# Attention in cycles of three score tiles, with the tiles for the maxima in a ring of four single PSUM banks

## The reference, cut to what matters

```python
B, T, C = x.shape                       # 4, 1024, 256
h = (x - mu) * rsqrt(var + 1e-05) * ln_gamma + ln_beta
qkv = (h @ w_qkv + b_qkv).reshape(B, T, 3, 16, 16)      # 16 heads of 16
scores = einsum('bhqd,bhkd->bhqk', q, k) / sqrt(16)
attn = softmax(scores, axis=-1)
out = einsum('bhqk,bhkd->bhqd', attn, v)
out = out @ w_out + b_out
return residual + out
```

## Time and profile before

| what | us |
|---|---|
| median of three runs | 1146.5 |
| the profiled execution | 1145.95 |
| its span, first to last instruction | 1143.9 |
| TensorE busy (1: busy time) | 1065.6 (93%) |
| VectorE busy | 999.5 (87%) |
| ScalarE busy | 808.9 (71%) |
| first tile for the maxima to last copy of `ps_o` | 104.4 to 785.6 |

### The profile page before, as it was taken

The page is one execution under the profiler, slowest core; times in us unless marked ns, Lnnn a source line. Parts: engine busy times, 40 slices in busy tenths (PEclk is TensorE's granted clock), DMA queues, the critical chain, the costliest instruction groups (busy, mean ns, idle before and its releaser), DMA issues.

```text
span 1143.9 us, 22167 instructions
## 1 busy us (share of the span) xinstructions
PE 1065.6 (93%) x8566; PEld 584.0 (51%) x8566; DVE 999.5 (87%) x1475; ACT 808.9 (71%) x1654; POOL 244.6 (21%) x345
## 2 busy tenths in 40 slices
PE   5997899999999999999999999997899998999995
PEld 4885333333333333333333333334667765888884
DVE  6786999999999999999999999943499998579887
ACT  4462388888888888888888888874567686343443
POOL 6421600000000000000000000102254333565643
PEclk9898699999999999999999999998999998899998
DMA  7595404413432440442243140212134325634321
GB/s 272 153 313 202 57 13 76 67 29 59 68 48 41 76 64 17 74 68 40 48 68 60 36 76 12 92 56 59 41 111 144 110 86 164 195 87 135 103 75 55
DMA packets 87332, 101.55 MB, mean 89 GB/s; under 512 B 21884, under 2 KB 57212, under 8 KB 87228
## 3 DMA queue, kind: packets, MB, share of 16 engines
q1 hardware_dynamic: 86396, 98.56, 36.2%
q10 hardware_dynamic: 832, 1.58, 0.4%
HBM read 55.09 MB, written 43.88 MB: 87 GB/s over the span
## 4 chain that ended last, share of the span: by engine, by line
PE 70%; DVE 14%; issue 3%; POOL 2%; ACT 1%; DMA 1%; SPq 0%; DVEq 0%; PEldq 0%; POOLq 0%; ACTq 0%
PE ps_o L785 25%; PE ps_s L773 19%; PE ps_m L762 10%; DVE maxes L705 3%; PE p_a L1330 3%; PE p_p L1756 2%; DVE p_q_c L1254 1%; DVE p_kv_c L1254 1%; PE p_a L1733 1%; DVE ln_stats L69 1%; PE p_t L1336 1%; DVE p_hid L81 1%; DVE zT_lo L2019 1%; PE p_p L1402 1%; DMA inverse<-inverse_sums 1%
## 5 line engine op out<-in xcount | busy, mean ns | idle before, releaser
L679 ACT ACTIVATE prob<-ps_s 128x512 f32<-128x512 f32 x1024 | 556.1, 597 | 117.8 <-PE ps_s L773 101.0
L705 DVE TENSOR_REDUCE maxes<-ps_m 128x2 f32<-128x1024 f32 x512 | 605.4, 1217 | 16.0 <-PE ps_m L762 12.7
L785 PE MATMUL ps_o<-prob,v_ones 128*32 128x256 f32 x4096 | 327.3, 391 | 7.6 <-issue 7.2
L773 PE MATMUL ps_s<-q_stack,k_stack 64*128 64x512 f32 x1024 | 260.6, 499 | 0.0
L762 PE MATMUL ps_m<-k_stack,q_stack 62*128 62x512 f32 x1024 | 218.9, 420 | 12.7 <-DVE maxes L705 9.0
L773 PEld LDWEIGHTS ps_s<-q_stack,k_stack 64*128 64x128 f32 x1024 | 98.8, 184 | 210.8 <-ACT prob L679 187.9
L785 PEld LDWEIGHTS ps_o<-prob,v_ones 128*32 128x32 f32 x4096 | 81.6, 108 | 191.5 <-issue 102.8
L638 POOL COPY v_ones<-v_all 128x512 f32<-128x512 f32 x16 | 9.9, 616 | 511.2 <-PE ps_o L785 511.2
L762 PEld LDWEIGHTS ps_m<-k_stack,q_stack 62*128 62x128 f32 x1024 | 100.8, 191 | 30.2 <-DVE maxes L705 23.1
L405 ACT ACTIVATE p_parts<-ps_qk,cols 128x512 fp32r<-128x512 f32 x32 | 22.0, 688 | 38.2 <-PE ps_qk L450 33.3
L1402 PE MATMUL p_p<-p_hT,w_p 128*128 128x512 f32 x96 | 42.7, 594 | 2.6 <-ACT p_hT L1167 2.6
(11 more groups left out here) (301 smaller groups left out, 1538.3 us busy)
## 6 DMA issues: line engine op xcount, KB each, us to landing
qk_parts<-p_parts SPq DMA_DIRECT2D x32, 512.0 KB, 7.2
q_stack<-qk_parts SPq DMA_DIRECT2D x96, 128.0 KB, 4.7
k_stack<-qk_parts SPq DMA_DIRECT2D x96, 128.0 KB, 7.7
oT<-o_sb SPq DMA_DIRECT2D x32, 256.0 KB, 4.2
x_all<-in_x_dram SPq DMA_DIRECT2D x8, 512.0 KB, 10.0
heads<-oT SPq DMA_DIRECT2D x16, 256.0 KB
inverse<-inverse_sums SPq DMA_DIRECT2D x16, 256.0 KB
out_dram<-x_all SPq DMA_DIRECT2D x7, 512.0 KB, 3.5
```

The costliest lines, as they stand in the source:

```text
L679: act.activation(prob[at % P_RING][:, h], ps_s[:, (GH * at + h) % S_RING], ACT.Exp, scale=HD ** -0.5).then_inc(exp_done, 1)
L705: dve.tensor_reduce(maxes[:, i // 2, i % 2], ps_m[:, i % M_PAIRS], AX.X, ALU.max).then_inc(m_taken, 1)
L773: pe.matmul(ps_s[:, (GH * (UNITS * slot + KT * qc + kt) + h) % S_RING], r32(k_st[slot][rows, pair, kt * P:(kt + 1) * P]), r32(q_st[slot][r ...
L785: ins = pe.matmul(ps_o[32 * h:32 * h + 32, queries], v_st[slot][:, kt, h], prob[(UNITS * slot + KT * qc + kt) % P_RING][:, h, queries], st ...
```

## The change

The work of attention is put into another order, and the two kinds of tiles are handled in other units.

- A cycle of TensorE now has three score tiles, three tiles for the maxima and three quarters of a block of products (`weigh` over 384 queries, or split over two blocks as 128 + 256 or 256 + 128), in the order s s m m s m, products. A half has ten such cycles and one of two tiles (`CYCLES` is 11, `tiles_of`). Products are those of two cycles earlier.
- `ps_m` is a ring of four single banks; TensorE waits for each tile, and VectorE reduces one bank (128 x 512 elements) with one instruction, 974 times; only in front of the loop, for 50 tiles, does it still take pairs (25 times). `maxima_through` turns a tile's number into the count of reductions.
- The rows of the array of the two kinds are swapped for the tiles for the maxima (`BASES[1 - i % 2]`), and `place_max` follows that.
- The chain of four small instructions of VectorE becomes: two maxima into `maxm` and `top`, a subtraction, a transpose. The signs change (the stack of keys gets -1 where it had 1). They are put behind the first, second and third reduction of the next half but one instead of following each other, and `maxes` has two buffers.
- The reciprocals, `take_o` (now after six exponentials of a half, before after four) and the steps of `begin_mixing` (now one in each cycle) take places in the new order.

```diff
-M_PAIRS = 2
-M_MMS = GH * (CHUNK // P) * (T // CHUNK)
-AHEAD = M_MMS // 2
+M_BANKS = 4
+TILES = GH * KT
+HALVES = NG * T // CHUNK
+CYCLES = TILES // 3 + 1
+LEAD = TILES + 18
+FIRST_PAIRS = LEAD // 2
+ALL_TILES = TILES * HALVES
+ALL_MAXIMA = FIRST_PAIRS + ALL_TILES - LEAD
+LAST_HALF = (ALL_TILES - LEAD) // TILES
+LAST_CYCLES = (ALL_TILES - LEAD) % TILES // 3 + 1
+
+def tiles_of(j):
+    return 3 if j < CYCLES - 1 else 2
+
+def maxima_through(tile):
+    return tile // 2 + 1 if tile < LEAD else FIRST_PAIRS + tile - LEAD + 1
...
+                        if half and GH * kt + h == 5:
+                            take_o(*divmod(half - 1, QC))
...
+            def take_max(tile, count):
+                half, i = divmod(tile, TILES)
+                bank = tile % M_BANKS
+                dve.wait_ge(m_ready, tile + count)
+                dve.tensor_reduce(maxes[half % 2][:, i:i + count], ps_m[:, bank:bank + count], AX.X, ALU.max).then_inc(m_taken, 1)
...
+            def whole_maxima(half):
+                dve.wait_ge(m_taken, maxima_through(TILES * half + TILES - 1))
+                for dst in (maxm[:], r32(top[:, 0])):
+                    dve.tensor_tensor(dst.rearrange("p (hp odd t) -> p hp t odd", hp=HP, odd=2), by_head(half)[:, :, :, 0], by_head(half)[:, :, :, 1],
+                                      ALU.max).then_inc(own, 1)
+
+            def low_parts(half):
+                dve.wait_ge(own, 3 * half + 2)
+                dve.tensor_tensor(top[:, 1], maxm[:], top[:, 0], ALU.subtract).then_inc(own, 1)
+
+            def turn_maxima(half):
+                g, qc = divmod(half, QC)
+                dve.wait_ge(own, 3 * half + 3)
                 dve.wait_ge(m_in[qc], 32 * g)
+                dve.transpose(topT[qc][:], top[:].rearrange("p a b -> p (a b)")).then_inc(m_turned, 1)
...
+            for half in range(HALVES):
+                for j in range(CYCLES):
+                    for tile in range(TILES * half + LEAD + 3 * j, TILES * half + LEAD + 3 * j + tiles_of(j)):
+                        if tile < ALL_TILES:
+                            take_max(tile, 1)
+                        if half + 1 < HALVES:
+                            past = tile - TILES * (half + 2)
+                            if past == 0:
+                                whole_maxima(half + 1)
+                            if past == 1:
+                                low_parts(half + 1)
+                            if past == 2:
+                                turn_maxima(half + 1)
+                    if half in (HALVES - 5, HALVES - 4) and j % 3 == 0:
+                        invert(4 * (half - (HALVES - 5)) + j // 3)
...
+            def fill_max(tile):
+                if tile >= M_BANKS:
+                    pe.wait_ge(m_taken, maxima_through(tile - M_BANKS))
+                score_for_max(tile, tile % M_BANKS).then_inc(m_ready, 1)
...
+            def weigh(half, first, count):
+                g = half // QC
+                while count:
+                    kt, at = divmod(first, GH)
+                    to = min(GH, at + count)
+                    n, queries = KT * half + kt, slice(at * P, to * P)
+                    if at == 0:
+                        pe.wait_ge(exp_done, GH * n + GH + S_RING)
+                        if kt == 0:
+                            pe.wait_ge(o_taken, half)
+                            pe.wait_ge(v_set, g + 1)
+                    for h in range(GH):
+                        ins = pe.matmul(ps_o[32 * h:32 * h + 32, queries], v_st[g % SLOTS][:, kt, h], prob[n % P_RING][:, h, queries],
+                                        start=kt == 0 and at == 0, stop=kt == KT - 1 and to == GH)
+                    if to == GH:
+                        ins.then_inc(pv_done, 1)
+                    first, count = first + to - at, count - (to - at)
...
+                for j in range(CYCLES):
+                    tile = TILES * half + LEAD + 3 * j
+                    score(half, 3 * j)
+                    score(half, 3 * j + 1)
+                    if tile + 1 < ALL_TILES:
+                        fill_max(tile)
+                        fill_max(tile + 1)
+                    if tiles_of(j) == 3:
+                        score(half, 3 * j + 2)
+                        if qc == 0 and tile + 2 == TILES * (half + 2) and tile + 2 < ALL_TILES:
                             pe.wait_ge(stack_in[nxt], STACK_LOADS * ((g + 1 - nxt) // 3 + 1))
+                        if tile + 2 < ALL_TILES:
+                            fill_max(tile + 2)
+                    slot = CYCLES * (half - LAST_HALF) + j - LAST_CYCLES
+                    if slot >= 0:
+                        begin_mixing(slot)
+                    weigh_cycle(half, j - 2)
```

More of the change, by code:

```diff
@@ L669, in take_o @@
                 act.activation(o_sb[qc][:], ps_o[:], ACT.Copy).then_inc(o_taken, 1)
[L671 to L689, removed]
+            for half in range(HALVES):
+                for kt in range(KT):
+                    n = KT * half + kt
+                    act.wait_ge(pv_done, n)
+                    for h in range(GH):
+                        act.wait_ge(s_ready, GH * n + h + 1)
+                        act.activation(prob[n % P_RING][:, h], ps_s[:, (GH * n + h) % S_RING],
+                                       ACT.Exp, scale=HD ** -0.5).then_inc(exp_done, 1)
+                        if half and GH * kt + h == 5:
+                            take_o(*divmod(half - 1, QC))
             take_o(NG - 1, 1)
@@ L698, in invert @@
                 dve.reciprocal(sums[:, at], sums[:, at]).then_inc(inverted, 1)
[L700 to L716, removed]
-                dve.wait_ge(m_in[qc], 32 * g)
-                dve.transpose(negT[qc][:], neg[:].rearrange("p a b -> p (a b)")).then_inc(m_turned, 1)
@@ L767, in score, with score_for_max @@
-            def score(g, slot, qc, kt, h):
-                n = UNITS * g + KT * qc + kt
-                if h == 0 and kt == 0:
+            def score_for_max(tile, bank):
+                half, i = divmod(tile, TILES)
+                g, qc = divmod(half, QC)
+                hp, t, kc, base = i // 16, i // 4 % 4, i // 2 % 2, BASES[1 - i % 2]
+                q0 = qc * CHUNK + t * P
+                return pe.matmul(ps_m[:, bank], r32(q_st[g % SLOTS][base:base + MROW, hp, q0:q0 + P]),
+                                 r32(k_st[g % SLOTS][base:base + MROW, hp, kc * CHUNK:(kc + 1) * CHUNK]), start=True, stop=True)
@@ L791, in weigh_last @@
-            def weigh_last(g, u, qc, kt, half, first):
-                if kt:
-                    weigh(g, u, qc, kt - 1, half)
-                elif qc:
-                    weigh(g, u, 0, KT - 1, half)
-                elif not first:
-                    weigh(g - 1, (u - 1) % SLOTS, QC - 1, KT - 1, half)
-            def scores_ahead(g, u, qc, kt, pair, last):
-                nxt = (u + 1) % SLOTS
-                if 2 * kt < KT:
-                    to, i0 = ((g, u, 1) if qc == 0 else (g + 1, nxt, 0)), AHEAD + 4 * kt
-                else:
-                    to, i0 = (g + 1, nxt, qc), 4 * kt - AHEAD
-                if not (last and to[1] == nxt):
-                    for i in range(2):
-                        score_for_max(*to, i0 + 2 * pair + i)
+                pe.wait_ge(exp_done, n + 1)
@@ L843, in on_tensor @@
[L843 to L854 removed]
+            Z_TURN = CYCLES * (HALVES - LAST_HALF) - LAST_CYCLES - CH
```

131 lines of the change are left out of this document (50 added, 81 removed).

## The result

The changed kernel takes 1127.34 us (median of four runs, 1126.37 to 1132.45), the kernel before on the same chip 1147.26; the ratio is 0.983, with a 95% interval of 0.980 to 0.986. That is 19.9 us or 1.7% less; 1128.4 was forecast.

What follows compares the result with a forecast made beforehand. TensorE bounded the kernel (20.24 us a half); VectorE would become the bound at 19.52. The last reduction 17.6 us earlier, no gain in the tail: 1145.95 - 17.6 = 1128.4 us; forecast 1121 to 1133 (0.52), wider range 1114 to 1145.

Steps and rivals of the forecast that it cites:

- What bounded the kernel before: Attention loop: TensorE's chain of 1.24 us a pair cycle sets the end, 19.84 of 20.24 us a half, VectorE 6% behind.
- TensorE's cycle of three: TensorE in the attention loop: 1.69 us a cycle against 1.86 for one and a half pair cycles; 18.4 us a half.
- ScalarE's loop: Exponentials through the ring of three: 1.74 us a cycle; with the `ps_o` copy and TensorE, 18.9 to 19.0 us a half.
- The step that carries the forecast: VectorE in attention: a 512-element reduction takes 0.598 us, bounds 0.566 and 0.61; 32 make 19.14 us a half.
- The rule that 512 elements from PSUM take 0.66 us: Skill page's estimate for VectorE reductions, giving 21.4 us a half; the prediction set it against the trace's 1.131 for 1024.
- The ring: Four banks for the maxima between TensorE and VectorE: margin 0.25 us a cycle, stalls 0.03 us a half.
- Way of the maxima: Maxima's way from DMA to landing: some 5 us against about ten until needed, so hidden with five to spare.
- The sum: Attention's total: last reduction ends at 733.7 instead of 751.3 us, 17.6 earlier; tail 34.1; whole 1128.4 us.
- Dearer cycle of TensorE: Rival 1, attention loop: middle pair, splits or ring cost more; up to 20.1 us a half, 1133 to 1145; chance 0.19.
- dearer reduction: Rival 3, VectorE's fixed part larger: decides from 0.621 us; at 0.658 the whole takes 1187 us; chance 0.05.
- ring without margin: Rival 4: VectorE waits every cycle for the first tile; with 0.15 us, 21.2 a half, 1178 us; chance 0.08.
- The rival that the fixed part of a reduction is smaller: Rival 2, VectorE: at 0.566 us a reduction TensorE with ScalarE bounds at 18.95 a half, 1111 us; chance 0.09.

Runs made afterwards that it cites:

- VectorE relieved: Kernel before, each pair reduction reading 2 x 256 of 2 x 512 keys: 1136.32 us; changed kernel, single reductions reading 256 of 512: 1104.12 us.
- the kernel with four score banks: Changed kernel with reductions over 256 of 512 keys, all single, and one PSUM bank moved from the maxima to the scores: 1084.65 us.
- the kernel with short reductions: Changed kernel, each single reduction reading only the first 256 of its 512 keys: 1104.12 us, ratio 0.963.
- the kernel with pairs: Changed kernel's cycle of three, but VectorE reduces two banks with one instruction all the way: 1241.8 us.
- the first profile: Profiled execution of the changed kernel in its first measurement, the longest of four runs: 1132.45 us, span 1130.4.
- the second: Profiled execution when the changed kernel was run again with no edit: span 1125.9 us; that measurement 1128.25 us, ratio 0.983.

## Why the prediction was right

**What bounded the kernel before.** Right: TensorE's order of 1.24 us a pair. With VectorE relieved the half stayed at 20.13, as worked out, and nothing but the small chain's 0.1 went.

**TensorE's cycle of three.** 1.69 us was worked out from rows of a cycle of two, and 1.69 stands in the kernel with four score banks. That the middle pair would overlap, which no row had shown, is so (0.24), but only with the rows of the array swapped: the kernel without the swap pays some 0.22 in each cycle of three. One term was wrong: products split over two blocks cost nothing, not 0.05 each, so TensorE's half is 15.21 + 1.45 + 1.46 = 18.1 and not 18.4, the copy of `ps_o` left aside.

**ScalarE's loop.** The mechanism was right, its sizes off: the ring of three costs 0.29 a half and the copy of `ps_o` 0.33. Together with TensorE 18.73, where I had 18.9 to 19.0. This changed nothing in the forecast, since VectorE stood above it, but made the kernel with short reductions 7 us faster than I expected.

**VectorE.** The step that carries the forecast: 0.598 us for a reduction of 512 elements, taken from two instructions of another kind at 0.59 and 0.61; measured 0.597. The small group 0.38, measured 0.38; with a half at 19.48 (19.52 worked out) and the shares of the windows, VectorE as the new bound is shown twice over: taking load away brings the time down at once (24 us, 4 to 5 us), adding 0.26 a half brings 7.8 us. The reciprocals cost 3.2 us in their three halves where 3.7 were worked out, and they had not been quite covered before (0.7 us in two halves). That 0.597 came within 0.001 of the value taken is in part luck: its two source rows differ by 0.02, and 0.024 more would have been the whole gain. The rule that 512 elements from PSUM take 0.66 us did not hold for reductions that follow each other. The Trainium skill, "VectorE: DVE Perf Modes", section on the TRN2 errata, gives 120 cycles plus one for each element; the 0.597 measured back to back leaves 0.06 us beside 512 elements at its 0.96 GHz, half of that fixed part. As the duration of one instruction it is near: 0.68 us in the profile, of which the next one overlaps 0.08. Had it held as the interval, the change would have been slower: at 0.621 the gain is gone.

**The ring.** Its margin was worked out as 0.25 us a cycle. In the loop of the changed kernel no reduction waits (924 of them from 160 to 725 us, no idle time), so the margin was enough; how much of it is left wasn't measured. That the pieces of the ring decide is shown by the kernel with pairs: 23.34 us a half, inside the 23 to 23.5 expected.

**Way of the maxima.** Hidden in the loop, as said, but not in the last half, where five to spare was wrong. TensorE waits there 0.2 us in the first profile, 1.5 in the second and 2.5 in the kernel with short reductions. In the first profile the sync queue issues the load of the maxima 3.3 us after their store in the loop (421.15, 424.43), and 5.5 us after it ahead of the last half (716.59, 722.12), a few us behind its DMAs for the sums. What makes it later there wasn't tested.

**The sum.** From the first reduction to the end of the last the sum had 628.7 us; two executions took 626.6 and 628.8. The tail, 34.1 worked out, took 33.8. Attention as a whole gave 20.2 us back in the first execution and 17.9 in the second; 17.6 were forecast. The parts around it took 6.7 us in the first execution: 2.6 ahead of attention through a wait for a DMA, and 4.1 behind it. The second has 0.8 less ahead of attention than the kernel before, and 0.7 more behind it. The median, 1127.34, is 1.1 under the forecast; that it is so close is luck in part, since the four runs of this one kernel spread over 6 us.

**The rivals.** Dearer cycle of TensorE, dearer reduction, ring without margin: none came. Two of them come with one edit: rows not swapped 20.48 a half, pairs in the ring 23.34. The dearer reduction only the measured 0.597 rules out. The rival that the fixed part of a reduction is smaller was wrong in its price, too; up to 0.75 a half would have been to gain, not 0.57.

## What to carry to other kernels

When several engines are near full, write the sum of each for one unit of work, and ask of a change which sum it moves: here all but VectorE became 1.4 us a half shorter (20.13 to 18.73, with VectorE relieved in both kernels), which was worth 0.75, because 1.0 more for reductions on VectorE met it, and the price of an instruction of half the size decided it with a margin of 0.02 us. Changes between kinds of tiles cost TensorE about 0.1 us each here, so longer runs of a kind pay, if the ring between the engines is cut into pieces as fine as the new rhythm needs. Once an engine has no pause left, its small instructions are time: two of 0.08 us a half were 4 to 5 us, and four in one piece instead of between reductions were 7.8.

## What the runs showed of the hardware

- Two matrix products over 64 rows each that start on different halves of the array's rows start together (403.10 and 403.10) and cost one stream; on the same half the second starts 0.24 us later (403.27 and 403.51), and the cycle is some 0.22 longer. The order 0 1 1 0 0 1 overlaps as well as 0 1 0 1.
- Tiles of one kind follow each other after 0.24 us; where products follow instead it is 0.33, and behind products the first pair needs 0.34. These three held, to 0.01, wherever TensorE waited for nothing. The Trainium skill, "TensorEngine Tiling (Array Packing)", section Key Properties, says that changing the tiling mode drains TensorE; the 0.1 us more at each change between products and the other two kinds agrees with it, but no run shows what it consists of.
- Splitting products of 384 queries into 128 and 256 cost nothing (0.79 us either way).
- Four small VectorE instructions that wait for each other stand 0.20 to 0.22 us apart; placed between reductions three of them take 0.08 or 0.09 us each and the transpose 0.13.
- Two executions of the same kernel had spans of 1130.4 and 1125.9 us: 3.4 us came off ahead of attention, where one DMA was waited for 5.1 us in the first, 3.4 behind it, and attention itself took 2.3 us more.
